# Two-layer graph network kernel: the first layer's two stores of a step are issued from ScalarE's queue instead of SyncE's

## The reference, cut to what matters

```python
h = jnp.maximum(_layernorm(x, axis=-1), 0.0)
x = x + _L0_gnn_ref(h, edge_attr_4, edge_attr_8, ...)
h = jnp.maximum(_layernorm(x, axis=-1), 0.0)
x = x + _L1_gnn_ref(h, node_vec1, src, dst, edge_attr_4, edge_attr_10, ...)

# inside a layer
xs_e, xv_e = xs[src], xv[src]                       # gather the source node of each edge
msg = ...  # products of gathered features, edge harmonics and w = MLP(edge_embed)
agg = jax.ops.segment_sum(msg, dst, num_segments=n)
out = agg @ W2 + s @ Wsc                            # then gates (layer 0 only) and the residual
```

## Time and profile before

| | |
|---|---|
| median of 3 runs | 2620.4 us (2619.82 to 2622.44) |
| the profiled execution: time, span | 2619.57 us, 2617.8 us |
| PE / PEld busy | 2413.1 us (92%) / 2317.7 us (89%) |
| DVE / ACT / POOL busy | 2346.5 (90%) / 1909.4 (73%) / 1954.0 (75%) us |
| DMA: mean rate | 129 GB/s |
| TensorE's granted clock, mean | 0.981 of 2.4 GHz |

### The profile page before, as it was taken

How to read it: one execution, slowest core, us unless ns; L and a number is a source line. 1 busy time by engine, 2 the same in 40 slices (tenths; PEclk the granted TensorE clock), 3 DMA queues, 4 the chain that set the end, 5 groups by cost and what they waited for, 6 DMA issues and landing times. The chain is left out here.

```text
span 2617.8 us, 93014 instructions
## 1 busy us (share of the span) xinstructions
PE 2413.1 (92%) x27323; PEld 2317.7 (89%) x27323; DVE 2346.5 (90%) x10157; ACT 1909.4 (73%) x5020; POOL 1954.0 (75%) x2035
## 2 busy tenths in 40 slices
PE   0599999999999999999999999489999999999996
PEld 0499999999999999999999999389999999999996
DVE  7599999999999999999999998179999999999995
ACT  1499999999999999999999999234444444444442
POOL 3688888888888888888888887156666666666661
PEclk9999999999999999999999999689999999999998
DMA  5244444444444444444444443156666666666662
GB/s 139 67 117 119 121 119 117 121 119 117 123 119 115 122 121 116 121 119 118 122 118 119 120 119 98 39 135 169 170 170 164 165 163 164 164 164 163 165 165 74
DMA packets 564122, 337.83 MB, mean 129 GB/s; under 512 B 220808, under 2 KB 546036, under 8 KB 563493
## 3 DMA queue, kind: packets, MB, share of 16 engines
q1 hardware_dynamic: 462385, 216.12, 32.5%
q0 software_dynamic: 48736, 83.76, 12.8%
q10 hardware_dynamic: 52500, 32.01, 4.0%
HBM read 199.56 MB, written 132.08 MB: 127 GB/s over the span
## 5 line engine op out<-in xcount | busy, mean ns | idle before, releaser
L690 POOL DMA_INDIRECT xg<-in_x,win x501 | 720.4, 1438 | 159.9 <-issue 147.6
L690 POOL DMA_INDIRECT xg<-sources,win x501 | 556.2, 1110 | 354.4 <-issue 167.3
L1175 PE MATMUL out_ps<-w_out,aggT 128*100 128x64 f32 (+2 forms) x6012 | 620.8, 253 | 1.8 <-ACT aggT L1010 1.2
L1175 PEld LDWEIGHTS out_ps<-w_out,aggT 128*100 128x100 f32 x6012 | 593.5, 168 | 3.6 <-issue 2.2
L1161 PE MATMUL agg_ps<-sel,msg 128*128 128x100 f32 x4512 | 574.2, 277 | 5.5 <-DVE msg L848 5.4
L1161 PEld LDWEIGHTS agg_ps<-sel,msg 128*128 128x128 f32 x4512 | 536.9, 193 | 7.0 <-DVE msg L848 7.0
L1010 ACT COPY aggT<-agg_ps 128x600 f32<-128x600 f32 x377 | 248.0, 658 | 125.7 <-PE agg_ps L1161 92.0
L702 POOL TENSOR_TENSOR rs<-ve,neghalf 128x4 f32<-128x4 f32 x251 | 271.5, 1082 | 20.9
L976 ACT ACTIVATE hn<-xn,nmr,rs 128x192 f32<-128x192 f32 x501 | 244.1, 535 | 57.5 <-DVE nmr L791 57.5
L996 ACT COPY xw_sb<-xw_ps 128x192 f32<-128x192 f32 x251 | 80.1, 319 | 271.1 <-PE xw_ps L1149 271.1
L1032 ACT ACTIVATE h<-xo,nmr,rs 100x192 f32<-100x192 f32 x501 | 246.7, 541 | 2.8 <-DVE nmr L896 2.8
(11 more groups left out here) (157 smaller groups left out, 5774.6 us busy)
## 6 DMA issues: line engine op xcount, KB each, us to landing
sources<-ev SPq DMA_DIRECT2D x250, 250.0 KB
xn<-in_x SPq DMA_DIRECT2D x250, 125.0 KB
xmid<-xo SPq DMA_DIRECT2D x250, 125.0 KB
ev<-xmid SPq DMA_DIRECT2D x250, 125.0 KB
ev<-sources SPq DMA_DIRECT2D x250, 125.0 KB
out<-xo ACTq DMA_DIRECT2D x250, 125.0 KB
win<-edge_rec SPq DMA_DIRECT2D x1002, 3.5 KB
ee_sb<-ee_parts SPq DMA_DIRECT2D x501, 18.0 KB
```

The costliest lines, as they stand in the source:

```text
L690: pool.indirect_dma_start(out=xg[:, t.slot, j, 0:D], out_offset=None, in_=edge_rows, in_offset=bass.IndirectOffsetOnAxis(ap=win[:, t.slot, ...
L1175: ins = pe.matmul(rows[0:NT, j, c0:c1], aggT[:, t.half, j, k, :], w[f"out{k}_"][:, :], start=fresh, stop=True, skip_group_check=not fresh)
```

## The change

The two stores of a step move from the end of SP's step to ACT's step, behind `hidden_act` of `T(1)`. They stay stores of `T(9)` and keep their wait on `ev_ready`. In the pass over single tiles, the second layer's two loads of old rows (`ev`) move from the inner loop over chunks to the outer one over tiles, ahead of the edge loads, and the wait of `add_base` counts them per tile.

```diff
@@ SP, step
-                if (t := T(PRE + 1)) and first:
-                    sp.wait_ge(ev_ready, t.m + 1)
-                    sp.dma_start(rows_of(new_dram, t), xo[0:NT, t.slot, :, 0:D]).then_inc(stored[t.slot], 16)
-                    sp.dma_start(rows_of(sources, t), ev[0:NT, t.slot, :, :, :].rearrange("p j k c -> p j (k c)")).then_inc(stored[t.slot], 16)
@@ SP, second pass, load(f)
                 sp.dma_start(long_a[:, :], node_col[bass.ds(tile * NT, NT), :]).then_inc(base_in, 16)
+                if not first:
+                    sp.dma_start(ev[0:NT, RING, 0, 0, :], node_rows[bass.ds(tile * NT, NT), :]).then_inc(xn_in[RING], 16)
+                    sp.dma_start(ev[0:NT, RING, 0, 1, :], sources[bass.ds(tile * NT, NT), D:2 * D]).then_inc(xn_in[RING], 16)
@@ DVE, add_base
-                dve.wait_ge(xn_in[t.slot], (t.uses + 1) * 32)
+                dve.wait_ge(xn_in[t.slot], (t.m - (NB - 1)) * 32 if t.serial else (t.uses + 1) * 32)
@@ ACT, step
                 if t := T(1):
                     hidden_act(t)
+                if (t := T(PRE + 1)) and first:
+                    act.wait_ge(ev_ready, t.m + 1)
+                    act.dma_start(rows_of(new_dram, t), xo[0:NT, t.slot, :, 0:D]).then_inc(stored[t.slot], 16)
+                    act.dma_start(rows_of(sources, t), ev[0:NT, t.slot, :, :, :].rearrange("p j k c -> p j (k c)")).then_inc(stored[t.slot], 16)
```

More of the change, by code:

```diff
@@ L667, in chunk @@
                 sp.reg_add(edge, edge, P)
[L668 to L671, removed]
+                if first:
+                    sp.dma_start(xn[0:NT, t.slot, 0, 0:D], node_rows[bass.ds(tile * NT, NT), :]).then_inc(xn_in[t.slot], 16)
             def finish(t, record, f):
```

## The result

The changed kernel takes 4430.8 us (median of 4 runs, 4429.4 to 4433.4), beside 2620.1 us for the kernel before (4 runs, 2619.5 to 2622.4). The ratio is 1.6909, with a 95% interval of 1.688 to 1.6938. I forecast 3671 us (3555 to 3955). The direction and the place of the new wait were right. The size was off by 760 us: 1811 us were lost, and I had counted 1051.

What follows compares the result with a forecast made beforehand. PE was taken to bound the kernel before, with DVE and ACT within 6%. Seven terms summed to a 10.51 us step against 6.17; over 242 turns that adds 1050 us, plus 1, to 2619.6: 3671 us, range 3557 to 3954.

Steps and rivals of the forecast that it cites:

- terms 4 and 5: First layer, ACT: `hid` released in 0.04 us; first store then issues at once, the second 0.36 us later.
- rival A: First layer, ACT's queue: the store passes the waiting `hid`; cycle 9.24 us, time 3363 us; chance 0.07.
- term 6: First layer: the second store lands 3.2 us after its issue, near the drain's 3.1 us.
- my upper bound of 4.0: First layer, second store's landing: at most 4.0 us, including an estimated 0.7 us for a tail.
- term 1: First layer, DVE's own work from `residual` to the end of the line writing `he`: 5.52 us, kept as before.
- terms 2 and 3: First layer: PE sees `he` in about 0.05 us, then its transposes through the closing matmuls take 1.24 us.
- The dense part has cover: First layer, PE: 4.7 us of work (9.4 at lower clock) fits in 9.2 us between `hid` and the next transposes.
- the clock comes back in the dense part: First layer, PE: clock falls in pauses and recovers in the dense part behind `hid`, with PE 57% busy.
- Rival B: First layer, PE: the clock never recovers; 12.0 us per step, at least 4031 us; chance 0.08.
- my 1050: First layer: 242 turns, each 4.34 us longer because `residual` waits for the store, cost 1050 us.

Runs made afterwards that it cites:

- fill: Changed kernel plus 36 small bf16 matmuls per first-layer turn in PE's pause ahead of `outputs`, results overwritten; two runs, 3761 and 3909 us.
- rows_first: Changed kernel with `new_rows` of `T(6)` ahead of `residual` of `T(2)` on DVE; 3703.9 us, ratio 1.4137.
- late_on_sp: Kernel before, both stores still on SP's queue, but the store of turn t made to wait for `hid` of turn t + 8; 4453.1 us, ratio 1.6996.

## Why the prediction was wrong

**Right.** L771 waits for the store in 242 turns. The store leaves 0.05 us behind the end of L1125, with `hid`, so it does not pass this waiting `hid` (terms 4 and 5, rival A out). The second store is 0.33 behind the first (0.36 forecast) and lands 3.25 later (3.2 forecast, term 6). That term 6 fits is in part luck: in rings of about the forecast's own length the landing took 3.90 (fill) and 3.94 us (rows_first), with means of 4.07 and 4.32 that lie above my upper bound of 4.0. SP's wait for `ev` is gone, the second layer's steps are the same, and ACT's 0.58 of issuing is hidden by DVE's wait. DVE's own work from L771 to the end of L761 is 2018.38 - 2012.87 = 5.51 (5.52 forecast, term 1).

**Wrong, first step: terms 2 and 3.** I closed the ring through `he`: DVE ends L761, PE transposes it, then L1125. `edge_h` works on `T(0)` and the transposes on `T(1)`, so there is a turn of slack between them. The two lines in the changed kernel, from the start to 2021.3 us, show it:

```profile
L761 DVE TENSOR_TENSOR he<-xg,mv x148: 546/550/558, 91.0 to 2017.8; 128x384 f32<-128x384 f32 x148
```

```profile
L1110 PE MATMUL hT_ps<-ident,he x439: 270/421/474, 91.6 to 2021.3; 128*128 128x128 f32 x147
```

The transposes of `he` are three in a turn, and 439 is 3 x 146 + 1, so the one that starts at 2021.29 is of the 147th turn. The `he` of 2017.83 is already the 148th. The one that L1110 reads was written a whole step of 13.6 us earlier. I had the two offsets in the text about the kernel and did not subtract them. DVE's part is not what the ring of the changed kernel waits for. It is in rows_first, but by way of L853.

**Wrong, second step: "The dense part has cover".** This is the step that cost the size. I put 4.7 us of PE's work (9.4 at the lower clock) anywhere in the 9.2 us between `hid` and the next L1109, as if it could run while the store lands. It can't: `outputs` waits for L863, which waits behind L771 in DVE's queue. Only the `sums` (L1162) run during the landing. All the rest, from L1176 to L1125, comes behind the landing, so it is on the ring in full, and a lower clock lengthens it in full. rows_first shows the link: with it taken away, L1176 starts while the store is under way, and 727 us come back, the higher clock's part included.

**Wrong, third step: the clock comes back in the dense part.** It came back too late to help. The first row is from the start of L1176 to the end of L1125 in another step of the changed kernel, the second from there to the next L1176 (columns as in the earlier trace rows):

```profile
705.76:714.69 8.93, 8.93 (x66) 8.36 (x67) 4.88 (x26) 3.21 (x8) 4.62 (x6) 0.50 0.12 26
714.69:719.29 4.60, 1.66 (x13) 1.52 (x13) 1.06 (x3) 2.81 (x7) 0.00 (x0) 0.87 0.37 110
```

PE's part of the ring runs at 0.50 throughout. The clock rises only in the `sums` behind it and stays up through most of PE's pause, and by the next L1176 it has fallen again. In the step of 2009 us it did not rise at all. From 500 to 3300 us, some 205 steps, it rose 152 times, each time behind the end of L1125. So it did alternate in many steps, but the stretches that lift the mean from 0.50 to 0.59 begin outside PE's part of the ring, and in that part PE needed 8.92 us for 5.14 us of work. Rival B, with 0.08, came nearest in this. Its time ("at least" 4031 us) was of a PE that is the limit, and here PE pauses. I argued against it that PE would hardly pause at the lower clock. But PE's pause was not what its own work left over. It was a wait for the landing, which stays however slowly PE works. The Trainium skill describes such a case on its page "TensorE: Matmul & The Clock Gate" (section "HAM oscillation — how this bites in real kernels"): a kernel whose PE waits for a transfer in every tile pays for the clock again in each. I had not weighed it. The trace agrees that a recurring wait costs the clock, with 0.59 in the window above and 0.97 once the wait was filled. It differs in that PE's work is the longer part here, 80% of the time.

**Where the 1811 us went.** The ring at full clock, read from fill, is 10.48 us, so 242 x (10.48 - 6.17) = 1043 us is the lateness. That this is my 1050 is chance, for the path is another. The lower clock adds 242 x (13.61 - 10.48) = 757 us, which is 3.78 us more of PE's work and 0.65 less of landing per turn. Together 1800 us. The split leans on one execution of fill, whose landing is not that of the changed kernel. With the mean of fill's 170 full-clock steps from 500 to 2500 us, 10.67 us, in place of the one step, it is 1089 and 714 us, so it is good to some tens of microseconds.

**Still open.** Why a 250 KB store takes 3.25 to 3.34 us to land in the slow steps (the changed kernel, late_on_sp) and 3.90 to 3.94 in the faster ones (fill, rows_first, in the steps shown) was not separated from what else moves at the time. The DMA rate was 54 GB/s in the first and 68 to 69 in the second.

## What to carry to other kernels

When a store that frees a ring slot moves, compare by turn count the slot's next writer with the instruction that the store now stands behind. Here it was the same turn, so the landing of a transfer became part of every step, whichever queue issues it. Then list what is queued behind the waiting instruction and who waits for each of these, and subtract the turn offsets of writer and reader before calling a link tight: one line behind `residual` held PE, and the `he` that I took for the link had a turn to spare. Work that starts only when the wait is over must be priced at both levels of the clock. And where a store is to be issued from a compute engine, put it where released work is queued around it (2 us here), not where the engine would next start something (107 us, in the run with a turn of slack).

## What was not expected of the hardware

- PE was 80% busy in the first layer and the granted clock still stood at a mean of 0.59, with one pause of 2.7 us in the mean in each 13.6 us. Matmuls of no use in that pause raised it to 0.97 and made the kernel 522 to 670 us faster.
- Where the clock did come back, it rose near the end of PE's busy stretch, stayed up while PE paused, and was down again when PE went on (705.76 to 719.29 us).
- At the lower clock the same stretch of PE's work took 1.74 times as long (8.92 against 5.14 us, or 1.79 without the 0.17 us pause in the latter), not twice.
- Two DMA issues on ACT's queue left no idle time on ACT where released instructions run beside them, and 0.58 us where both stand directly behind `hid`, with nothing released between it and them.
